# The message product in three f32r passes in place of plain fp32

## The reference, cut to what matters

```
x_conv = transpose(relu(bn(conv17(relu(bn(conv1(xc))))) + xc))
s = x @ w_se.T + b_se                 # 3 columns
dist = sq[:, :, None] + sq[:, None, :] - 2 * einsum('bnd,bmd->bnm', s, s)
A = exp(-dist) * mask                 # mask is adj
msg = relu(x @ w_msg.T + b_msg)       # 128 columns
x_nmp = einsum('bnm,bmd->bnd', A, msg)
gi = concat([x_conv, x_nmp]) @ w_ih.T + b_ih
gh = x @ w_hh.T + b_hh
r, z = sigmoid(gi_r + gh_r), sigmoid(gi_z + gh_z)
y = layernorm(x + (1 - z) * tanh(gi_n + r * gh_n) + z * x)
h = (1 + eps) * y + einsum('bnm,bmd->bnd', adj, y)
out = layernorm(y + relu(h @ W1 + b1) @ W2 + b2)
```

## Time and profile before

| | |
|---|---|
| median of 3 runs | 415.11 us (414.59 to 415.78) |
| the profiled execution, its own time | 415.75 us |
| its span, first to last instruction | 413.9 us |
| PE busy | 380.0 us (92%) |
| PE weight loads busy | 338.3 us (82%) |
| DVE busy | 309.7 us (75%) |
| ACT busy | 211.1 us (51%) |
| POOL busy | 224.3 us (54%) |
| message product, matmul instructions | 128 in all, 16 in a group |

### The profile page before, as it was taken

One profiled execution on the slowest core, in us unless ns is written; L12 is line 12 of the kernel. 1 busy time (PEld: TensorE's weight loads), 2 busy tenths in 40 slices (PEclk: granted clock), 3 DMA queues, 4 the chain that ended last, 5 costly groups with the idle time before them and its releaser, 6 DMA issues.

```text
span 413.9 us, 6658 instructions
## 1 busy us (share of the span) xinstructions
PE 380.0 (92%) x2369; PEld 338.3 (82%) x2369; DVE 309.7 (75%) x599; ACT 211.1 (51%) x366; POOL 224.3 (54%) x215
## 2 busy tenths in 40 slices
PE   2479999998999999998999999999999999999974
PEld 1478888898898898988898988988988988989864
DVE  3878847879588885888688795878768795867665
ACT  3637456642755337443566427653484436461641
POOL 2536544848357464657349473565556573495252
PEclk9989999999999999999999999999999999999999
DMA  7302001110012000130012010120001300000101
GB/s 270 155 2 102 2 1 51 41 64 25 26 52 103 24 29 0 53 101 25 25 51 73 29 44 7 51 101 25 27 6 46 104 25 28 1 2 0 52 0 51
DMA packets 7561, 19.40 MB, mean 47 GB/s; under 512 B 625, under 2 KB 4977, under 8 KB 6385
## 3 DMA queue, kind: packets, MB, share of 16 engines
q1 hardware_dynamic: 7392, 19.02, 13.2%
q10 hardware_dynamic: 144, 0.07, 0.1%
HBM read 14.89 MB, written 4.19 MB: 46 GB/s over the span
## 4 chain that ended last, share of the span: by engine, by line
PE 57%; DVE 23%; issue 8%; POOL 5%; ACT 4%; DMA 2%; SPq 0%; DVEq 0%; POOLq 0%; ACTq 0%
PE back L1074 28%; PE conv L1074 14%; PE back L1236 6%; DVE tail L882 5%; POOL rstd L472 4%; PE front L1149 3%; DVE xn L882 3%; PE front L1121 2%; DMA tail<-in_conv_dram 2%; DVE esum L839 2%; DVE usum L843 2%; DVE usum L827 2%; DVE wl L925 1%; DVE stats L872 1%; DVE stl L765 1%
## 5 line engine op out<-in xcount | busy, mean ns | idle before, releaser
L1074 PE MATMUL conv<-sth,wh 128*128 128x256 f32 x320 | 99.5, 311 | 16.5 <-DVE stl L765 13.1
L1074 PE MATMUL conv<-stl,wh 128*128 128x256 f32 x320 | 92.8, 290 | 0.0
L1074 PE MATMUL conv<-sth,wl 128*128 128x256 f32 x320 | 92.7, 290 | 0.0
L1074 PEld LDWEIGHTS conv<-sth,wh 128*128 128x128 f32 x320 | 62.2, 194 | 20.6 <-DVE wl L925 10.4
L472 POOL TENSOR_TENSOR rstd<-rstd,minus_half 128x4 f32<-128x4 f32 (+1 forms) x34 | 36.1, 1062 | 65.2 <-DVE rstd L876 65.2
L1074 PEld LDWEIGHTS conv<-stl,wh 128*128 128x128 f32 x320 | 62.3, 195 | 1.0
L1074 PEld LDWEIGHTS conv<-sth,wl 128*128 128x128 f32 x320 | 62.1, 194 | 0.0
L477 POOL TENSOR_TENSOR xw<-xw,xv 128x512 f32<-128x512 f32 (+1 forms) x17 | 20.9, 1228 | 62.0 <-ACT xw L640 62.0
L490 POOL TENSOR_TENSOR amat<-amat,adjT 128x512 f32<-128x512 f32 x32 | 48.1, 1525 | 5.1 <-ACT amat L616 4.2
L882 DVE TENSOR_SCALAR tail<-tail,stats,rstd 128x128 f32<-128x128 f32 x64 | 41.4, 709 | 0.0
L647 ACT ACTIVATE xch<-usum 128x512 fp32r<-128x512 f32 x16 | 10.1, 631 | 40.7 <-DVE usum L843 40.7
(11 more groups left out here) (198 smaller groups left out, 987.1 us busy)
## 6 DMA issues: line engine op xcount, KB each, us to landing
adjT<-in_adj_dram SPq DMA_DIRECT2D x8, 1024.0 KB, 4.8
out_dram<-tail SPq DMA_DIRECT2D x15, 256.0 KB, 2.2
xv<-in_x_dram SPq DMA_DIRECT2D x7, 512.0 KB, 3.3
tail<-in_conv_dram SPq DMA_DIRECT2D x1, 1088.0 KB, 8.2
gbuf<-in_gates_dram SPq DMA_DIRECT2D x1, 576.0 KB, 11.8
xv<-in_x_dram SPq DMA_DIRECT2D x2, 256.0 KB, 3.0
later_w<-in_later_dram SPq DMA_DIRECT2D x1, 452.0 KB, 8.9
out_dram<-tail SPq DMA_DIRECT2D x2, 128.0 KB, 1.9
```

Source lines behind the costliest of these rows:

```text
L1074: ins = pe.matmul(bank, a, b, start=first and k == 0, stop=last and k == len(todo) - 1)
```

## The change

The message product becomes three f32r instructions for each block, `xh` with `wmh`, `xh` with `wml` and `xl` with `wmh`, with 132 moving columns each. `wmh` and `wml` are the high and low parts of `wmsg_se`, made once in the prologue. ACT makes `wmh` between the two h1 outputs and the first tap copy, after a wait for the load of `later`; DVE makes `wml` ahead of `tap_low(0)`. PE waits for `wml` in place of the load. DVE's own wait for `later` goes away. W1 moves from the `later` load (452 KB before, less 128 KB) to the `gates` load (576 KB before, more 128 KB) and so into `gbuf`, and `msum` moves by two slots in it.

```
-    o["gates"] = np.concatenate([hh, ih[:, 1], ih[:, 0]], axis=1)
+    w1 = f["L1_gnn_W1"].reshape(P, HID // P, P)
+    o["gates"] = np.concatenate([hh, ih[:, 1], ih[:, 0], w1], axis=1)
...
+        wmh = sb("wmh", [P, MSGW], f32r)
+        wml = sb("wml", [P, MSGW], f32r)
...
-        graw, msum = gslots[:, 0:9, :], gslots[:, 9:9 + NM, :]
+        gw1raw, graw, w1raw = gslots[:, 0:11, :], gslots[:, 0:9, :], gslots[:, 9:11, :].rearrange("p k o -> p (k o)")
+        msum = gslots[:, 11:11 + NM, :]
...
-                sp.dma_start(graw, t["gates"]).then_inc(gates_loaded, 16)
+                sp.dma_start(gw1raw, t["gates"]).then_inc(gates_loaded, 16)
...
                 h1_out(0, 0)
+                act.wait_ge(later_loaded, 16)
+                act.activation(wmh[:, :], wmsg_se, ACT.Copy).then_inc(w_msg_high, 1)
                 act.wait_ge(tap_sums, 1)
                 tap_high(0)
...
+                dve.wait_ge(w_msg_high, 1)
+                dve.tensor_tensor(wml[:, :], wmsg_se, full(wmh[:, :]), ALU.subtract).then_inc(w_msg_low, 1)
                 tap_low(0)
                 odd_low(0, 0)
                 tap_low(1)
                 tap_low(2)
                 diff_low(0, 0)
-                dve.wait_ge(later_loaded, 16)
                 dve.wait_ge(factors_set, 2)
...
-                        ins = pe.matmul(m[:, q - q0, :], xv[u][:, c:c + P], wmsg_se, start=True, stop=True)
+                        ins = products(m[:, q - q0, :], [(xh[u][:, c:c + P], xl[u][:, c:c + P], wmh[:, :], wml[:, :])])
...
                 taps(0, 1)
-                pe.wait_ge(later_loaded, 16)
+                pe.wait_ge(w_msg_low, 1)
                 messages(0, 0)
```

More of the change, by code:

```diff
@@ L67, in laid_out @@
     hh = f["L0_gnn_w_hh"].reshape(3, P, P).transpose(2, 0, 1)
-    o["gates"] = np.concatenate([hh, ih[:, 1], ih[:, 0]], axis=1)
+    w1 = f["L1_gnn_W1"].reshape(P, HID // P, P)
+    o["gates"] = np.concatenate([hh, ih[:, 1], ih[:, 0], w1], axis=1)
     o["later"] = np.concatenate([f["L0_gnn_w_msg"].T, f["L0_gnn_w_se"].T, np.zeros((P, 1), np.float32),
-                                 np.tile(f["L0_gnn_b_se"], (P, 1)), np.zeros((P, 1), np.float32), f["L1_gnn_W1"],
+                                 np.tile(f["L0_gnn_b_se"], (P, 1)), np.zeros((P, 1), np.float32),
                                  f["L1_gnn_W2"].reshape(2, P, D).transpose(1, 0, 2).reshape(P, 2 * D),
@@ L100, in gnn_kernel @@
         c1raw = first_w[:, NVEC:NVEC + P]
-        W1_AT = MSGW + 4
-        W2_AT = W1_AT + HID
+        W2_AT = MSGW + 4
         later_w = sb("later_w", [P, W2_AT + 2 * D + 2 * P])
@@ L105, in gnn_kernel @@
         bse = later_w[:, MSGW:MSGW + NSE]
-        w1raw = later_w[:, W1_AT:W1_AT + HID]
         w2 = later_w[:, W2_AT:W2_AT + 2 * D].rearrange("p (f d) -> p f d", d=D)
@@ L278, in gnn_kernel @@
         w_low = sem("w_low")
+        w_msg_high = sem("w_msg_high")
+        w_msg_low = sem("w_msg_low")
         def wait(eng, name, g, j):
```

## The result

The kernel after takes 425.03 us (median of 4 runs, 423.36 to 425.40), the kernel before 415.39 us beside it (4 runs). The ratio is 1.0245, 95% interval 1.0212 to 1.0277: slower by 2.1 to 2.8%. A ratio is estimated from all the executions and need not equal the quotient of the two medians. The profiled execution took 425.23 us with a span of 422.9 us: 9.5 us more in time and 9.0 us more in span than the one before.

A forecast was written before the change was run, and what follows sets the result against it. PE was taken as the bound, with the message slot on the period's chain of waits. Seven steady slots (6.2 us) plus the prologue (about 1.05) gave 7.3 us on 415.75 or the median 415.11; forecast 422.6 us, range 416.5 to 427.

The forecast's parts named there:

- its own case: Whole kernel: the outcome as forecast, 421 to 425 us, chance 0.64.
- the main term: Message slot on PE: the f32r step; 0.06 to 0.07 or 0.22 us would break the forecast there.
- The step: Message product on PE: each 132-column f32r instruction takes 0.112 us, read as its weight load; 24 take 2.69 us.
- The steady slots: Message slots of the 7 steady groups: each grows 0.89 us and delays the gates on PE, 6.2 us in all.
- DVE in the steady slot: Vector chain behind the messages: not delayed by itself; third bank full at 103.65 us, DVE comes at 103.80 anyway.
- The preparation: Prologue: DVE's subtraction for the low weights adds 0.23 us; ACT's high copy is hidden, ending near 11.8 us.
- Group 0: Prologue: group 0's message slot feeds DVE directly and grows by 0.89 us, of which +0.8 us was counted.
- the clock: Whole run: no term of the sum; 0.50 only in 28 to 31 us, where a phase change may move some tenths.
- Narrow f32r did not fall back to two fp32 steps for each product: Message slot: rival that each narrow f32r product costs two 0.112 us steps, slot 5.4 us, about 444 us; chance 0.16.
- the columns did not set the step: Message slot: rival that only columns set the step, 0.06 to 0.068 us, total about 412.3 to 414.0; chance 0.04.
- the added time was not absorbed: DVE or POOL stretch: rival that its slack hides half of each slot's 0.89 us, about 418.7 us; chance 0.09.
- loads did not overlap further: Message slot: rival that loads overlap in part, step 0.088 us, slot 2.11 us, about 417.8 us; chance 0.07.

The follow-up runs named there:

- one-pass kernel: The kernel after with only the high-times-high pass, 8 instructions in a slot and both corrections left out: 410.29 us against 415.26, ratio 0.987.
- preparation-only kernel: The kernel after with the message product in plain fp32 as before, its weight preparation and moved W1 kept: 415.74 us against 415.26, ratio 1.0019.
- the fill: 18 throwaway f32r products ahead of PE's last long wait: added to the kernel after 422.29 us, to the kernel before 414.09, each against 415.27.
- two-pass kernel: The kernel after without its third pass (low x times high weights), 16 f32r instructions in a slot: 416.81 us against 415.26, ratio 1.0018.

## Why the prediction was right, and what it had too small

- **The total.** Forecast 422.6 us, measured 425.03. It lies in the range of 416.5 to 427, but 0.03 us over the 421 to 425 that the prediction gives for its own case: the main term held, and a wide range took in what the sum had left out.
- **The step.** Forecast 0.112 us, measured 0.112 (2.68 us for 24). The three experiments that change columns and instructions apart from each other agree: fewer columns with as many instructions change nothing, nearly as many columns with fewer instructions give the time back, and 16 f32r instructions cost what 16 fp32 ones do. So the count sets the slot, and not the columns. Every instruction here has a weight load of its own, so the counts do not tell the load from another fixed cost of an instruction. Two rows speak for the load: the loads after a pause are 0.11 us apart with no product ahead of them, and the distance products of the kernel after, whose weights fill 32 of the 128 rows, show that an instruction as such can start sooner. Four of their loads, the last of them 0.18 us long, take 0.30 us: two start within 0.01 us of each other at 126.40 us, the other two at 126.51, one step of 0.11 us later:

```profile
126.40 0.30 PEld L1148 LDWEIGHTS front<-factT 32*128 32x128 f32 x4
```

No kernel here uses loaded weights twice, so full loads are not taken out by any run, and how the loads and products take turns inside PE is not shown.
- **The steady slots.** Forecast +0.89 us for each of 7. The slot grew by 0.88 and the period by 0.83: 244.1 us in five of them, where the chain of before has 340.91 - 100.96 = 239.95. This is the step of the sum that carries 6 of the 7.3 us, and it held. The slot is on the path nearly in full; the one-pass kernel shows it from the other side (0.96 for 0.90). The odd 0.05 us is no more than the period moves with the slot left in fp32: 47.93 us in the preparation-only kernel, 47.99 before.
- **DVE in the steady slot.** DVE takes the first bank at 105.12 us right behind its tail normalization, without a wait, as forecast.
- **The preparation.** Forecast +0.23 us. The subtraction keeps DVE from its next one for 0.21 us (12.65 to 12.86); the medians differ by 0.5 us, with an interval from 0.0 to 1.6 us. ACT's copy starts when the load of 324 KB lands, after 7.5 us, and ends at 10.5 us, ahead of the tap copy at 11.56, which waits 1.07 us more for the tap sums. It was hidden, as forecast:

```profile
10.17 0.31 ACT L679 ACTIVATE wmh<-later_w 128x132 fp32r<-128x132 f32 x1 [1.54 <-DMA later_w<-in_later_dram]
11.56 0.74 ACT L665 ACTIVATE wh<-adjT 128x640 fp32r<-128x640 f32 x1 [1.07 <-DVE adjT L965]
```

- **Group 0.** Forecast +0.8 us for its slot. In the second profile of the kernel after, without slow steps in it, 0.94 us arrive; in the first, 1.7, of which 0.9 are the nine slow steps.
- **The term that was too small: the clock.** The forecast was 7.3 us, and the medians differ by 9.6. In the spans of the first profiles, the first slot starts 0.1 us earlier, group 0 to group 1 adds 1.7 us, the periods up to the last slot add 5.0, and the tail adds 2.4, of which 0.9 are the last slot and 1.5 the fall of the clock: 9.0 together, 2.4 of them by the clock. Another 0.5 us of the two profiled executions lies outside their spans; its cause is open. The prediction said of the clock that it was no term of the sum and might move the time by some tenths; it read 0.50 only in 28 to 31 us, though the steps in the first taps are slow up to 21.0 us as well, where the views print 1.00. The stretches do more: 1.5 us in this tail, and single executions of the kernel before spread from 411.7 to 417.6 us. Both low stretches appear in kernels with the fp32 slot as well, so they are no consequence of the f32r form as such. Without the fill, the fall in the tail stood in 6 of 7 profiles of kernels with an f32r slot (not in the one with group 0 in fp32) and in 2 of 3 of those with the fp32 slot. Whether the change makes such falls more frequent, and so costs a part of the 2 us beyond the slots, these few profiles can't settle.
- **The rivals.** None of them came. Narrow f32r did not fall back to two fp32 steps for each product (444 us), the columns did not set the step (412 to 414 us), the added time was not absorbed beyond 0.05 of 0.88 us in a slot, and loads did not overlap further (417.8 us). The 81 ns that the Trainium skill gives for a pair at 128 columns (TensorE: Matmul & The Clock Gate, "Back-to-back issue gap") is not what these rows show; f32r with 132 columns steps by 112 ns.

## What to carry to other kernels

Count the instructions, not only the columns: where each product loads 128 columns of 4-byte weights of its own, a step does not fall under 0.11 us here, and three f32r passes at that floor beat two fp32 instructions only when an fp32 step is over one and a half times it, 0.17 us. With 132 columns they lose by 3 to 2. With 256, three steps of 0.12 us are 0.36 us, and two fp32 steps of (1.89 - 0.38) / 7 = 0.216 us (the aggregation above) are 0.43; that is an estimate, since no kernel here ran the aggregation in three passes. A product on the path of a repeating period should be priced by its step and multiplied by the periods; and a loss of some tenths of a per cent should be compared over enough runs that the phase of the clock averages out.

## What the runs showed of the hardware that was not expected

- At the low level of the clock the f32r step with 132 columns is 0.21 us (21.89 to 22.11 us; 22.23 to 22.44 us in the two-pass kernel, granted 0.50), the same as that of 256 columns there (21.57 to 21.78), and 0.11 us at the high one. So the floor nearly doubles when the clock halves: it goes with PE's clock, and a 132-column product costs as much there as a 256-column one.
- Around PE's wait of 2.5 us in the tail the granted clock falls in some executions and not in others of the same kernel: behind it in the kernel after (wait over at 404.95 us, low from 405.8), within it in the second profile of the kernel before (low from 394.6, wait over at 395.18). With throwaway products in the wait, none of the four kernels that had them showed slow steps behind it.
- The stretches at the low level in the first 35 us begin and end at other times in each execution (the slow steps in the first taps ended between 17.5 and 23.5 us), and the first steady slot started between 50.1 and 54.4 us.
